# A convolution and mixture-of-experts kernel on one core: layer 1's input made first in each step, the routing's sums and prefix moved, filter matrices placed by the host, buffers aligned

## The reference

```
def _layer(x, style, w, b, mw, mb, typ):
    s = style @ mw.T + mb
    weight = SCALE * w * s[:, None, :, None]
    demod = lax.rsqrt(jnp.sum(weight * weight, axis=(2, 3)) + EPS)
    weight = weight * demod[:, :, None, None]
    ...            # same: 3 taps; upsample: transposed, stride 2, then blur; downsample: blur, then stride 2
h = x
for i, typ in enumerate(('same', 'upsample', 'same', 'downsample')):
    h = _layer(h, cond_512, weights[i], biases[i], mod_w[i], mod_b[i], typ)
t = h.reshape(-1, 512)                                   # 4096 tokens
scores = sigmoid(t @ gate_w.T) + bias
topk_w, topk_idx = top_k(scores, 4);  topk_w /= sum(topk_w) + 1e-20
out = sum over the 4 experts of topk_w * (silu(t @ Wg.T) * (t @ Wu.T)) @ Wd.T
out += (silu(t @ Sg.T) * (t @ Su.T)) @ Sd.T              # shared expert
return x + out
```

## Time and profile before

| | |
|---|---|
| median of 3 runs | 1250.92 us (1247.87 to 1251.91) |
| the profiled execution's own time | 1250.38 us |
| its span in the trace | 1248.7 us |
| granted TensorE clock, mean | 0.973 |
| busy: PE, DVE, POOL, ACT | 1139.2, 804.7, 574.0, 501.1 us |

### The profile page before, as it was taken

How to read it: one execution, slowest core, us unless ns; L and a number is a source line. 1 busy time by engine, 2 the same in 40 slices (tenths; PEclk the granted TensorE clock), 3 DMA queues, 4 the chain that set the end, 5 groups by cost and what they waited for, 6 DMA issues and landing times. The chain is left out here.

```text
span 1248.7 us, 24559 instructions
## 1 busy us (share of the span) xinstructions
PE 1139.2 (91%) x7160; PEld 1002.9 (80%) x7161; DVE 804.7 (64%) x1979; ACT 501.1 (40%) x1164; POOL 574.0 (46%) x667
## 2 busy tenths in 40 slices
PE   3699999999999898765999999999999999999995
PEld 2477777777777777644999999999998899999995
DVE  6556777777777777655565565656557665555653
ACT  4455555655555555322232332333233332222321
POOL 1000151424233332364665656566656566666663
PEclk9999999999999998966999999999999999999998
DMA  4455444454444453214767676676766776665664
GB/s 148 128 177 144 136 135 138 135 148 135 135 135 141 131 140 110 77 34 135 158 124 151 112 154 124 152 118 117 155 115 159 186 142 136 115 113 109 114 112 74
DMA packets 141626, 162.43 MB, mean 130 GB/s; under 512 B 33120, under 2 KB 98720, under 8 KB 140064
## 3 DMA queue, kind: packets, MB, share of 16 engines
q0 software_dynamic: 35696, 74.34, 32.6%
q1 hardware_dynamic: 104608, 87.78, 23.8%
q10 hardware_dynamic: 1296, 0.01, 0.1%
HBM read 73.41 MB, written 55.18 MB: 103 GB/s over the span
## 5 line engine op out<-in xcount | busy, mean ns | idle before, releaser
L1253 PE MATMUL bank<-xt_hi,wup_hi 128*128 128x256 f32 x1104 | 275.4, 282 | 1.8 <-issue 1.7
L1253 PE MATMUL bank<-xt_hi,wup_lo 128*128 128x256 f32 x1104 | 275.1, 282 | 0.0
L477 POOL DMA_INDIRECT out_rows<-yb,sid x140 | 226.5, 1618 | 91.7 <-DVE yb L1036 68.5
L418 POOL DMA_INDIRECT lists<-entry,place x128 | 129.1, 1009 | 237.3 <-DVE place L863 188.6
L560 ACT ACTIVATE t<-bank,cB,cA 128x256 f32<-128x256 f32 (+1 forms) x384 | 173.9, 530 | 116.1 <-PE bank L217 112.9
L1253 PEld LDWEIGHTS bank<-xt_hi,wup_hi 128*128 128x128 f32 x1104 | 209.4, 190 | 6.5 <-issue 3.7
L1253 PEld LDWEIGHTS bank<-xt_hi,wup_lo 128*128 128x128 f32 x1104 | 208.9, 189 | 2.7
L464 POOL DMA_INDIRECT xg<-h_rows,gid x140 | 142.3, 1016 | 120.3 <-PE bank L1231 76.7
L1257 PE MATMUL bank<-xt_lo,wup_hi 128*128 128x256 f32 x1104 | 176.2, 281 | 0.0
L1036 DVE TENSOR_SCALAR yb<-bank,all_lists 128x512 f32<-128x512 f32 x138 | 100.0, 748 | 85.2 <-DMA out_rows<-yb,sid 51.0
L1257 PEld LDWEIGHTS bank<-xt_lo,wup_hi 128*128 128x128 f32 x1104 | 150.9, 189 | 0.0
(11 more groups left out here) (212 smaller groups left out, 2182.9 us busy)
## 6 DMA issues: line engine op xcount, KB each, us to landing
x<-x1p SPq DMA_DIRECT2D x64, 384.0 KB
wraw<-in_Wup SPq DMA_DIRECT2D x11, 1024.0 KB, 7.4
xraw<-in_xq SPq DMA_DIRECT2D x32, 260.0 KB, 3.9
xbase<-in_x SPq DMA_DIRECT2D x32, 256.0 KB, 2.7
h_rows<-hrow SPq DMA_DIRECT2D x128, 64.0 KB, 1.7
out_rows<-orow SPq DMA_DIRECT2D x32, 256.0 KB, 2.1
x<-x1p SPq DMA_DIRECT2D x64, 127.0 KB
wdraw<-in_Wdn SPq DMA_DIRECT2D x11, 512.0 KB, 9.5
```

The source lines that it names most:

```text
L418: pool.indirect_dma_start(out=lists, out_offset=bass.IndirectOffsetOnAxis(ap=place[:, home, r, k:k + 1], axis=0), in_=entry[:, home, r, k, ...
L477: pool.indirect_dma_start(out=out, out_offset=bass.IndirectOffsetOnAxis(ap=sid[:, u:u + 1], axis=0), in_=yb[:, u, :], in_offset=None, comp ...
L1253: pe.matmul(dst, lhs[a], rhs[0], start=k == 0 and a == 0, stop=False)
```

## The change

Six things, without their reasons:

- The host lays the filter matrices out (`placed_taps`, 20 matrices of 128 x 128) and sends taps, scales and biases as `taps` and `small`. DVE only mixes four of them into each of layers 1 and 3 (`mixture`), the blocks in `big` and PE's transposes of them are gone. The raw taps and 8 matrices lie in `yb` and `xg`, the experts' row buffers, and the other 12 in `placed`.
- At the start POOL scales groups 0 and 1 before it waits for the fill; constants are made later on DVE, and layers 0 and 2 have their matrices before layers 1 and 3.
- On DVE `layer0(g + 1)` stands first in the body; on SP `stack(g + 1)` comes before the h writes, and the load of `xraw` comes last.
- On PE the prefix stands behind layer 3. `settle` keeps the sums and `pos`; the rest is `places`, at the end of the body with `choose` and `mark`, behind `orow`.
- In bodies 32 and 33 logits, scores and routing come before the end of the shared expert.
- Buffers of 2048 bytes and more in a partition start on multiples of 512 bytes, others on multiples of 64.

```diff
+        filled = [FIRST_FREE]
+
         def sb(name, shape, dt=F32):
+            size = 2 if dt == BF16 else 4
+            for n in shape[1:]:
+                size *= n
+            gap = -filled[0] % (512 if size >= 2048 else 64)
+            if gap:
+                ctx.enter_context(nc.sbuf_tensor(f"{name}_gap", [P, gap // 4], F32))
+            filled[0] += gap + -(-size // 32) * 32
...
+        placed = [xg[:].rearrange("p u (t m) -> p (u t) m", m=P), sb("placed", [P, PLACED - PLACED_DOWN, P])]
+        wtap, wsq = [yb[0:C, u, 0:NL * C * K].rearrange("i (l o k) -> i l o k", l=NL, o=C) for u in range(2)]
...
+        MATRICES = ((placed[0], 0, FIRST, 2), (placed[0], 2, SAME, 2), (mixed, 0, UP, 1), (mixed, 1, DOWN, 3))
...
-            for q in range(Q):
-                sp.dma_start(wnat[C * q:C * q + C].rearrange("o l i k -> o l (i k)"),
-                             cw.rearrange("l o i k -> o l (i k)")).then_inc(S["taps_loaded"], 16)
             sp.dma_start(xraw[:, 0], xq[0]).then_inc(S["x_loaded0"], 16)
+            sp.dma_start(placed[0][:, PLACED_UP:PLACED_DOWN], placed_taps[:, PLACED_UP:PLACED_DOWN]).then_inc(S["placed_loaded1"], 16)
+            sp.dma_start(placed[1][:], placed_taps[:, PLACED_DOWN:]).then_inc(S["placed_loaded2"], 16)
...
-                if within(g, 0, G - 3):
-                    sp.wait_ge(S["x0_hi"], g + 2)
-                    sp.wait_ge(S["x0_lo"], g + 2)
-                    sp.dma_start(xraw[:, 1 - odd], xq[bass.ds(g + 3, 1)].rearrange("a p b v -> p (a b) v")).then_inc(S[f"x_loaded{1 - odd}"], 16)
                 if within(g, 3, G + 3):
                     sp.wait_ge(S["o_ready"], g - 2)
                     sp.dma_start(out[bass.ds(P * (g - 3), P), :], orow[:, 1 - odd, :]).then_inc(S[f"o_written{1 - odd}"], 16)
                     if within(g, 3, G + 1):
                         sp.dma_start(xbase[:, 1 - odd, :], x_rows[bass.ds(P * (g - 1), P), :]).then_inc(S[f"base_loaded{1 - odd}"], 16)
+                if within(g, 0, G - 1):
+                    stack(g + 1)
                 if within(g, 1, G + 1):
                     sp.wait_ge(S["h_ready"], g)
                     for q in range(Q):
                         sp.dma_start(h_rows[bass.ds(P * (g - 1), P), q * (L // Q):(q + 1) * (L // Q)].rearrange("(b c) w -> c b w", b=NB),
                                      hrow[C * q:C * q + C, 1 - odd]).then_inc(S[f"h_written{1 - odd}"], 16)
-                if within(g, 0, G - 1):
-                    stack(g + 1)
+                if within(g, 0, G - 3):
+                    sp.wait_ge(S["x0_hi"], g + 2)
+                    sp.wait_ge(S["x0_lo"], g + 2)
+                    sp.dma_start(xraw[:, 1 - odd], xq[bass.ds(g + 3, 1)].rearrange("a p b v -> p (a b) v")).then_inc(S[f"x_loaded{1 - odd}"], 16)
...
+            pool.wait_ge(S["s_ready"], 1)
+            for g in range(2):
+                scaled(g, g % 2, g // 2)
...
+            act.dma_start(smalls[:], small).then_inc(S["bias_loaded"], 16)
+            act.dma_start(wtap.rearrange("i l o k -> i (l o k)"), taps.rearrange("i l o k -> i (l o k)")).then_inc(S["taps_loaded"], 16)
+            act.dma_start(placed[0][:, 0:PLACED_UP], placed_taps[:, 0:PLACED_UP]).then_inc(S["placed_loaded0"], 16)
+
+            def matrix_hi(n):
+                src, at, to, m = MATRICES[n]
+                act.activation(cwt[0][:, to:to + m], src[:, at:at + m], ACT.Copy).then_inc(S["wts_hi"], 1)
+
+            act.wait_ge(S["placed_loaded0"], 16)
+            for n in range(2):
+                matrix_hi(n)
...
+            mixture(placed[0], 0, 1, PLACED_UP, UPK, "placed_loaded1")
+            layer0(0)
+            mixture(placed[1], 1, 3, 0, BK, "placed_loaded2")
+            for n in range(2, 4):
+                matrix_lo(n)
...
-            def settle(number, home, many):
+            def settle(number, many):
...
-                step(dve.tensor_tensor(pos[:, 0:many], bank[7][:, 0:many * E].rearrange("p (r e) -> p r e", r=many),
-                                       every(region[:], many), ALU.add))
+                dve.tensor_tensor(pos[:, 0:many], bank[7][:, 0:many * E].rearrange("p (r e) -> p r e", r=many),
+                                  every(region[:], many), ALU.add).then_inc(S["pos_ready"], 1)
+
+            def places(number, home, many):
+
+                dve.wait_ge(S["pos_ready"], number)
...
+                def routing():
+                    if many:
+                        places(number, 2 if many == R else (number - ROUNDS - 1) % 2, many)
...
+                if within(g, 0, G - 1):
+                    layer0(g + 1)
...
-                if within(g, 0, G - 1):
-                    layer0(g + 1)
-                many, number = settled(g, it, u)
-                if many:
-                    settle(number, 2 if many == R else (number - ROUNDS - 1) % 2, many)
...
+                if many:
+                    settle(number, many)
+                if not conv:
+                    gathered()
+                    routing()
...
+                if conv:
+                    gathered()
                 if stage:
                     dve.wait_ge(S["down_done"], g - 1)
                     dve.wait_ge(S[f"base_loaded{odd}"], half(g, it, u, 2) * 16 + 16)
                     if not (early and g < 4):
                         dve.wait_ge(S[f"o_written{odd}"], half(g, it, u, 2) * 16)
                     dve.tensor_tensor(orow[:, odd, :], xbase[:, odd, :], bank[5][:], ALU.add).then_inc(S["o_ready"], 1)
+                if conv:
+                    routing()
...
-                many, number = settled(g, it, u)
-                if many:
-
-                    pe.wait_ge(S["mask_ready"], number)
-                    pe.wait_ge(S["zt_lo"], g - 2)
...
                     pe.wait_ge(S["x3_ready"], g * 4)
                     lo_passes(pe, dst, terms).then_inc(S["l3_done"], 1)
+                many, number = settled(g, it, u)
+                if many:
+
+                    pe.wait_ge(S["mask_ready"], number)
+                    pe.wait_ge(S["zt_lo"], g - 2)
+                    pe.matmul(bank[7][:, 0:many * E], tri[:], mask[:, 0:many], start=True, stop=False)
...
+                        logits()
                     pe.wait_ge(S["z_ready"], g - 1)
                     if many:
-                        pe.wait_ge(S["place_ready"], number)
+                        pe.wait_ge(S["pos_ready"], number)
```

More of the change, by code:

```diff
@@ L761, in first_in, with layer0 @@
                 minus(x0[1][:], xraw[:, par], x0[0][:]).then_inc(S["x0_lo"], 1)
+            for n in range(2):
+                matrix_lo(n)
             first_in(0, 0)
+            def layer0(g):
+                dve.wait_ge(S["t1_ready"], g + 1)
+                if not (isinstance(g, int) and g == 0):
+                    dve.wait_ge(S["x1_stacked"], g * (16 * STACKS))
+                dve.tensor_copy(x1p[:, 0], t1[:]).then_inc(S["x1_ready"], 1)
+                dve.wait_ge(S["x1_ready"], g * 2 + 1)
+                minus(x1p[:, 1], t1[:], x1p[:, 0]).then_inc(S["x1_ready"], 1)
             dve.wait_ge(S["sqrt_done"], 1)
@@ L1160, in body @@
                     lo_passes(pe, dst, terms).then_inc(S["l3_done"], 1)
+                many, number = settled(g, it, u)
+                if many:
+                    pe.wait_ge(S["mask_ready"], number)
+                    pe.wait_ge(S["zt_lo"], g - 2)
+                    pe.matmul(bank[7][:, 0:many * E], tri[:], mask[:, 0:many], start=True, stop=False)
+                    for r in range(many):
+                        if r:
+                            pe.matmul(bank[7][:, r * E:many * E], ones[:], mask[:, 0:many - r], start=False, stop=False)
+                        ins = pe.matmul(bank[7][:, r * E:r * E + E], ones[:], mask[:, R], start=False, stop=r == many - 1)
+                    ins.then_inc(S["prefix_done"], 1)
                 if stage:
@@ L1299, in _laid_out, with place @@
     xq = padded[:, :, :Q * (V + 2)].reshape(B // NB, NB, C, V + 2, Q).transpose(0, 4, 2, 1, 3).reshape(B // NB, P, NB, V + 2)
+    cw = inputs["L0_cond_weights"]
+    NL, _, _, K = cw.shape
+    def place(src, tap):
+        a = np.zeros((Q, C, Q, C), cw.dtype)
+        for q in range(Q):
+            for j in range(Q):
+                if 0 <= tap(q, j) < K:
+                    a[j, :, q, :] = src[:, :, tap(q, j)]
+        return a.reshape(P, P)
+    turned = cw.transpose(0, 2, 1, 3)
+    placed = [place(turned[0], lambda q, j: j + Q * m - q) for m in range(2)]
+    placed += [place(turned[2], lambda q, j: j + Q * m - q - 1) for m in range(2)]
+    placed += [place(cw[1], lambda q, j: 1 - 2 * j + q + n) for n in range(4)]
+    placed += [place(turned[3], lambda q, j: j + Q * m - 2 * q - n) for n in range(4) for m in range(3)]
+    small = np.concatenate([np.tile(inputs["L0_cond_mod_b"].T, (Q, 1)), np.tile(inputs["L0_cond_biases"].T, (Q, 1)),
+                            np.tile(inputs["L0_ffn_bias"], (P, 1))], 1)
     return {
```

258 lines of the change are left out of this document (104 added, 154 removed).

## The result

The changed kernel takes **1263.53 us** (median of 4 runs, 1261.13 to 1264.64) where the kernel before takes 1250.70 on the same chip (4 runs, 1247.87 to 1251.91): a ratio of 1.0078, 95% interval 1.0048 to 1.0109. It is slower, by 13 us. The profiled execution took 1264.64 us, with a span of 1262.8. The ratios in this document are of fast executions alone: one of experiment 3 and one of the kernel before beside experiments 1 to 4 were in a slower state and are left out of them, though not out of the medians.

The account below looks back on a forecast made before the run. PE was taken to bound the kernel, with some 21 us of waits in 380 in the convolution stage. Start -17.7, loop +24.6, last bodies -0.6 gave +6.3 on 1250.38: 1256.7, said 1256.5 us; range 1242 to 1270.

Parts of the forecast that it names:

- the forecast itself: Whole kernel: the prediction's own case, 1252 to 1262 us, chance 0.50.
- the wider 1242 to 1270: Whole kernel: range left without the first rival, the addresses and the dearer stall's far end; about 0.8.
- "slower": Whole kernel: time above the no-change band of 1247.2 to 1254.7 us, chance 0.49.
- The start: Start through group 2: layer 1 of group 0 near 26.9 us for 37.84, copy waits gone; together -17.7 us.
- The ordinary bodies: Convolution loop: bodies of 14.5, 14.85 and 14.6 us for u = 0, 1 and 2.
- The chain through `xt`: Loop bodies: ACT's `t1` and `t2`, DVE's splits and `xt_lo`, PE's up product; hardly any slack, holds the body.
- That `choose` and `mark` do: Loop, u = 1 and 2: one stands ahead of `x1p` and the splits, chain starts late; 14.85 and 14.6 us.
- The late place: Loop, u = 3: place 7.2 us later delays POOL, ACT and PE; 19.5 us in place of 14.68, six times.
- The clock: Behind each u = 3 stall: half clock for 3.4 us, costing 1.5 us, six times; bounds 0 and 3.4.
- the rival with the dearer stall: Loop: two stretches of half clock, or body 9's layers late as well; 1262 to 1274 us, chance 0.10.
- The last bodies: Layer 1 of group 29 to the last scatter's end: 87.4 us for 88.0, -0.6 us; bounds -8 and +5.
- Addresses: Buffer alignment: taken as 0; the rival that it makes PE faster, 1212 to 1245 us, had 0.05.

Follow-up runs that it names:

- experiment 3: Kernel before with only the place made late, behind `orow`, in the loop: 1300.08 us, ratio 1.0148 against the kernel before.
- experiments 1 to 4: Runs on one chip, where the kernel before takes 1279.9 us: three edits of the changed kernel and one of the kernel before; 1278.24, 1267.01, 1300.08, 1266.76 us.
- experiments 5 to 8: Runs on a second chip: kernel before 1281.58 us, changed kernel 1269.24, changed kernel with scaling first 1292.85, new start with old loop order 1277.55.
- experiment 12: Changed kernel with scaling first and scatters spread, plus SP issuing `xraw`'s load first in the body: 1259.42 us, ratio 0.9770 against the kernel before.
- Experiments 9 and 1: 9: changed kernel without the loop's scatters, 1230.25 us, ratio 0.9538. 1: changed kernel, POOL scaling before it waits for the place, 1278.24 us, ratio 0.9985.
- experiments 1 and 2: 1: changed kernel with POOL's scaling ahead of the place, 1278.24 us. 2: changed kernel with the place made early again, 1267.01 us, ratio 0.9903.
- Experiment 4: Changed kernel without the gaps that put buffers on 512-byte boundaries: 1266.76 us, ratio 0.9899 against the kernel before.
- experiment 11: Changed kernel with scaling first and each round's scatter groups spread over three bodies: 1251.35 us, ratio 0.9704 against the kernel before.
- experiment 7: Changed kernel with POOL's scaling ahead of the wait for the place, on a second chip: 1292.85 us, ratio 1.0066 against the kernel before.

## Why the prediction was right, and where not

The sum was 1256.5 us, and the forecast itself 1252 to 1262. The measured 1263.5 lies above that and inside the wider 1242 to 1270; "slower", given 0.49, is what came. The sign holds on the first chip; on the chip of experiments 5 to 8 the same change gives 0.9876. Nothing in the prediction told one chip from another. That the result was taken where PE's steps come in time is luck.

- **The start** was right in mechanism and size: layer 1 of group 0 at 26.96 (said: 26.9), group 5 sooner by 18.0 (said: 17.7), though 0.83 us of group 2's wait for the copies stay. The root ended at 11.85 (said: 11.8), the second split at 25.88 (25.6). The loads were hidden.
- **The ordinary bodies** are the term that was mis-sized. Measured 14.66, 15.27 and 14.96 us, said 14.5, 14.85 and 14.6: 0.9 us a round, 5.6 us in six. The chain through `xt`, named as the one with hardly any slack, holds PE for 8.0 + 3.2 us. That POOL's scaling beside DVE's cast makes it so is refuted by experiment 12. That `choose` and `mark` do, as the prediction had it, was not tried.
- **The late place** was right in its mechanism: place 3.4 us into the body (138.68 behind 135.24; said: 3.5), then 12.3 us of POOL, then ACT at once, then PE idle for 4.2 to 4.4 us (said: 4.7), six times. The body with the clock's part was said to be 19.5 + 1.5 = 21.0 us, and is 20.98, in part by luck, as the next point shows. Experiments 9 and 1 show the two links: without the scatters the u = 3 body lasts 15.40 us with the place as late as ever, and with the scaling ahead of them ACT no longer waits for POOL. What experiments 1 and 2 would take on the first chip was not measured, so that either would get the loss back there is argued from its traces.
- **The clock**: the stretches at 0.50 lasted 3.4 us twice and 6.8 us four times, not always one of 3.4. From the down product to the next layer 1 the six bodies take 1.3 to 2.4 us more than at full clock (2.89 us), 1.95 on the mean, where 1.5 was said. The down product came 17.55 us into the body, where 17.9 was said, and 0.2 was added for a late `zt_lo` that isn't seen. These misses of some 0.5 us cancel. The number also fell into the range of the rival with the dearer stall (1262 to 1274, 0.10). Its two stretches of half clock did come, four times in six, but the body was no dearer than said; the missing us lie elsewhere. The Trainium skill (TensorE: Matmul & The Clock Gate, "What's actually happening") has the array throttled unless activity releases it; the trace agrees, with 0.50 behind each of the six stalls.
- **The last bodies**: 573.82 - 486.61 = 87.2 us, said 87.4. Here too two misses cancel: the first single group's place came at 535.69, 1.8 us sooner than the working has it, and the 28 scatters behind took 37.3 us and not 35.7, since they had to wait once more for a place.
- **Addresses** were taken as 0. From the first expert's product to the last it was 655.8 us before and 658.2 after on the first chip, with 120.0 ns for 118.7. Experiment 4 finds 0.7 us between like kernels on one chip and no difference in the ratio that it could tell. So a changed spacing is real and its sum small; that the 2.4 us are due to it isn't shown.

Sum by steps: -18.0 + 30.1 - 0.8 + 2.4 + 0.4 at the very end = +14.1 us between the two profiled spans. Against the forecast's +6.3 the 5.6 us of the ordinary bodies and the 2.4 of the experts are what is missing.

What the prediction did not see at all is that PE's steps can arrive late while scatters run. It had no row for it: on the first chip that doesn't happen. On the others the kernel before takes 29 to 40 us more than there, and on one of them 45 less without the scatters. The changed kernel loses only some 6 (1269.24 for 1263.53). That turns the verdict.

What sets the chips apart, and by what path a scatter holds up PE's semaphore step, stays open. The runs show that scatters are needed for it, and that it is up to 2.5 us in runs of four (experiment 11) and up to 9.4 in runs of 12 (experiment 7). In those traces the steps of DVE and ACT come within 0.02 us of their instructions between 60 and 490 us; only those of PE are held.

## What to carry to other kernels

When a step is moved later, follow the in-order queue of the engine that consumes it: what stands behind it there, and who takes that. Here a 0.2 us `place` moved by 7 us cost some 33 us (six bodies of 20.98 us for 15.40 without scatters), through the queues of POOL and ACT. On chips like the last three here, keep runs of indirect transfers short and away from semaphore steps that something waits for at once. And compare on more than one chip before a per cent is believed: the same pair of programs gave 1.008 and 0.988. The lowest ratio here, 0.9704, came from spreading the scatters (experiment 11).

## What was not expected of the hardware

- Semaphore steps of PE's products arrive 3 to 9 us behind the product during 8 to 12 scatters of 128 entries in a row, on the three chips of the experiments; none in the two traces of the first comparison.
- The start-to-start spacing of the same matmuls follows buffer addresses: on one chip 118.4 and 120.4 ns for 128x256, 233.4 and 229.1 for 128x512, in opposite directions.
- A DVE cast of 128x512 took 1.26 us beside a scaling by POOL, and 0.43 alone:

```profile
134.87 0.43 DVE L944 CAST x_hi<-t 128x512 fp32r<-128x512 f32 x1
...
301.89 1.05 POOL L395 TENSOR_TENSOR xraw<-xraw,s 128x520 f32<-128x520 f32 x1 [6.70 <-DMA xraw<-in_xq]
301.96 1.26 DVE L944 CAST x_hi<-t 128x512 fp32r<-128x512 f32 x1
```
